# The weights of a two-layer kernel's mixtures: ScalarE issues their loads into six buffers, their splits move among the first scores, and the expert slots are cleared during the first mixtures

## Chip, core and metric

One core of one Trainium2 chip runs the whole program. The metric is the device time of one execution in microseconds. It is given as the median of several executions. Three executions of the kernel before gave 2954.35, 2950.48 and 2947.49 us.

## The reference

The input `x` is (32, 256, 256) float32 with a context of the same shape. There are four sublayers, each a normalisation followed by a block that is added to `x`:

```python
x = x + _L0_xattn_ref(_layernorm(x), ctx, ctx, Wq, bq, Wk, bk, Wv, bv, Wo, bo)   # 16 heads of 16
x = x + _L0_ffn_ref(_layernorm(x), P_w, U1, U2, U3, W1, W2, b2)
x = x + _L1_xattn_ref(_layernorm(x), ctx, ctx)                                   # no projections
x = x + _L1_ffn_ref(_layernorm(x), router_w, w_gate, w_up, w_down, ws_gate_up, ws_down)

def _mixture(inp, C, W):            # called with (x, C1, W1), then (gelu(.), C2, W2)
    for e in range(L):              # L = 12 matrices of 256 x 256
        y = y + C[:, e:e + 1] * (inp @ W[e].T)
```

The last block routes 8192 tokens to 8 of 64 experts. Each expert has 128 slots in a table in DRAM, and a token beyond an expert's capacity is dropped. A slot that nobody fills must read as zeros and must point at a spare output row.

## The kernel before

The 32 batches of 256 rows go through a pipeline that is written out by hand. Every step of a batch has a place on a scale of 40 units per batch (`PLACES`, `MIX`, `HALF_PLACES`). `pieces()` (lines 80 to 112) sorts all steps of all batches by place, and each of the five engines walks that one list and does its share of each step. So the list sets the order of the instructions on each engine, and semaphores keep the engines apart. A place is no time: an engine goes on as soon as what it waits for is there.

Products are done in fp32r with each operand in a high and a low part. For the weights, ScalarE rounds the float32 words to the high part (`split_hi`, line 592), and VectorE subtracts it from the words to get the low part (`split_lo`, line 753). There are 15 chunks of weights: three for the attention (`wo`, `wkv`, `wq`, `FIRST = 3`) and twelve for the mixtures, each two matrices and 128 x 1024 float32 large (512 KB). The raw words of a chunk land in a staging buffer. Two buffers exist: the last two of the five `x_mem` buffers, and `router_mem`. So chunk c is loaded when chunk c-2 has been split (semaphore `v_w`):

```python
def load_chunk(c):                                   # in sync_program, before
    if c >= 2:
        sp.wait_ge(v_w, c - 1)
    sp.e.dma_start(stage[c % 2][:, 0:chunks[c][2]], chunks[c][1]).then_inc(c_stage[c % 2], 16)
```

SyncE issues nearly all transfers of the kernel in the order of the list. Its queue also carries the stores of a batch's keys and queries (`k_parts`, `q_parts`), their rearranged loads (`spread`, from DRAM into `kst` and `qst`), and the four rows of maxima (`qst<-mT`) of each half. The steps `w_mix` (places 1, 3, 5, 11, ... 35) do three things in the kernel before: SyncE loads the next chunk and, for the first eight steps, clears the slots of eight experts by a transfer of 1284 KB (`expert_slots<-row_mem`, line 437), ScalarE splits, VectorE splits.

One half of an attention (8 heads, number `u`) is: `spread`; four `s1` steps (TensorE `first`, VectorE takes their maxima, `nm`, line 846); `max_rows` (VectorE `nmp`, TensorE turns them, ScalarE copies `mT`, SyncE spreads it); four `s2` steps (TensorE `second`, ScalarE `exps`, line 675); two `av` steps; `out_turn` (VectorE writes `ctx_o`). The first half of batch 0 begins at place 2.8 (its `spread`), its `s1` steps at 6.2 to 10.6, and its `s2` steps at 15.4 to 20.5. The mixtures of batch 0 stand at 53 to 88. In batch 1, places are 40 higher.

## Time and profile before

| | |
|---|---|
| median of three executions | 2950.48 us (2947.49 to 2954.35) |
| profiled execution | 2946.47 us, span 2944.7 us |
| TensorE matmuls busy | 2672.1 us, 91% of the span |
| TensorE weight loads | 2250.0 us, 76% |
| VectorE | 2222.4 us, 75% |
| ScalarE | 1060.2 us, 36% |
| GpSimd | 818.0 us, 28% |
| granted TensorE clock, mean over the span | 0.952 |
| moved by DMA | 327.29 MB, 111 GB/s over the span |

The span runs from the first to the last instruction that the profile shows. The time of the execution is 1.8 us longer. The profile's page also cuts the span into 40 slices of 73.6 us: TensorE is busy to 2 and 5 tenths in the first two, and to 9 or more from the third to about the 32nd.

### The profile page before, as it was taken

Reading aid. Unit: us, or ns where it says so; the run is one execution under the profiler, and the core shown is the slowest. Engines: PE = TensorE matmul, PEld = TensorE weight load, DVE = VectorE, ACT = ScalarE, POOL = GpSimd, SP = SyncE. Lnnn points to the kernel's source line nnn. Section 1 sums busy time; section 2 is a strip of 40 time slices with the busy share of each in tenths; the row PEclk is TensorE's granted clock in tenths of the full one; section 3 lists DMA queues with packets and bytes.
Section 4 is the critical chain, followed back from the end, with each engine's and each line's share of the span. In section 5 each row is a group of like instructions: output and inputs, shape, how many; then the busy total and the mean of one; then the engine's idle time right before and its main releaser. Section 6 shows DMA issues by size and latency. Waiting matters only on the chain. (4 is left out here: it accounts for less than half of the span.)

```text
span 2944.7 us, 60947 instructions
## 1 busy us (share of the span) xinstructions
PE 2672.1 (91%) x23496; PEld 2250.0 (76%) x23496; DVE 2222.4 (75%) x6041; ACT 1060.2 (36%) x1557; POOL 818.0 (28%) x862
## 2 busy tenths in 40 slices
PE   2599999999999999999999999999999999756886
PEld 1388888888888888888888888888888887636775
DVE  2478888888888888888888888888888887533332
ACT  1323444444344443444344433344444443211111
POOL 1000122232223322222222222222332222334334
PEclk6599999999999999999999999999999999857998
DMA  7624444444443344334344434333443331227886
GB/s 207 180 73 103 100 127 130 126 122 115 108 106 100 98 103 102 100 94 94 95 102 102 102 102 96 93 96 99 102 98 95 92 84 42 44 37 208 223 218 129
DMA packets 321061, 327.29 MB, mean 111 GB/s; under 512 B 45389, under 2 KB 302111, under 8 KB 320772
## 3 DMA queue, kind: packets, MB, share of 16 engines
q1 hardware_dynamic: 286980, 304.23, 40.3%
q0 software_dynamic: 33792, 19.17, 3.7%
q8 instruction: 186, 3.05, 0.5%
q14 instruction: 103, 0.84, 0.1%
HBM read 182.21 MB, written 212.37 MB: 134 GB/s over the span
## 5 line engine op out<-in xcount | busy, mean ns | idle before, releaser
L675 ACT ACTIVATE exps<-second 128x1024 f32<-128x1024 f32 x512 | 525.6, 1027 | 757.0 <-PE second L1172 732.7
L569 POOL DMA_INDIRECT expert_slots<-row_mem,sidx x512 | 506.9, 990 | 1005.1 <-PE first L1154 670.0
L1252 PE MATMUL mixp<-w_h,r_part_h 128*128 128x256 f32 x3072 | 667.6, 298 | 11.4 <-DVE hid L938 6.5
L846 DVE TENSOR_REDUCE nm<-first 128x4 f32<-128x1024 f32 x508 | 618.6, 1218 | 29.1 <-PE first L1154 25.6
L1252 PE MATMUL mixp<-w_h,r_part_l 128*128 128x256 f32 x3072 | 611.1, 280 | 0.0
L1252 PE MATMUL mixp<-w_l,r_part_h 128*128 128x256 f32 x3072 | 610.7, 280 | 0.0
L1252 PEld LDWEIGHTS mixp<-w_h,r_part_h 128*128 128x128 f32 x3072 | 468.6, 189 | 62.3 <-DVE hid L938 23.5
L1252 PEld LDWEIGHTS mixp<-w_l,r_part_h 128*128 128x128 f32 x3072 | 469.8, 189 | 0.0
L1252 PEld LDWEIGHTS mixp<-w_h,r_part_l 128*128 128x128 f32 x3072 | 469.7, 188 | 0.0
L938 DVE SCALAR_TENSOR_TENSOR x_mem<-mixp,C,x_mem 128x256 f32<-128x256 f32 x768 | 334.4, 477 | 77.6 <-PE mixp L1252 73.2
L938 DVE SCALAR_TENSOR_TENSOR hid<-mixp,C,hid 128x256 f32<-128x256 f32 x704 | 301.4, 476 | 108.4 <-PE mixp L1252 108.1
L1154 PE MATMUL first<-kst,qst 48*128 48x256 f32 x2032 | 238.9, 313 | 58.6 <-DVE nm L846 34.3
L538 POOL TENSOR_TENSOR norm<-norm,minus_half 128x2 f32<-128x2 f32 x128 | 92.0, 719 | 717.9 <-DVE norm L791 717.9
L1188 PE MATMUL attn_out<-exps,vx 128*17 128x256 f32 x4096 | 275.9, 392 | 11.1 <-issue 6.7
L1172 PE MATMUL second<-qst,kst 50*128 50x256 f32 x2048 | 237.4, 310 | 20.1 <-DMA qst<-mT 10.1
L1154 PEld LDWEIGHTS first<-kst,qst 48*128 48x128 f32 x2032 | 157.5, 189 | 111.4 <-DVE nm L846 37.8
L1172 PEld LDWEIGHTS second<-qst,kst 50*128 50x128 f32 x2048 | 159.1, 189 | 77.3 <-issue 30.4
L1188 PEld LDWEIGHTS attn_out<-exps,vx 128*17 128x17 f32 x4096 | 95.5, 98 | 112.1 <-issue 33.9
L582 POOL DMA_INDIRECT out<-x_mem,sidx x64 | 99.2, 1550 | 169.1 <-DVE sidx L1028 117.9
L681 ACT COPY out_sb<-attn_out 128x512 f32<-128x512 f32 x128 | 74.5, 582 | 133.3 <-PE attn_out L1188 117.3
L610 ACT ACTIVATE nat_h<-misc,qk_cols 128x256 fp32r<-128x256 f32 x128 | 53.8, 471 | 157.5 <-PE misc L1125 157.5
L813 DVE TENSOR_SCALAR xhat<-x_mem,norm 128x256 f32<-128x256 f32 x192 | 92.8, 524 | 9.2 <-issue 7.5
(223 smaller groups left out, 3620.0 us busy)
## 6 DMA issues: line engine op xcount, KB each, us to landing
kst<-k_parts SPq DMA_DIRECT2D x256, 192.0 KB
qst<-q_parts SPq DMA_DIRECT2D x256, 192.0 KB
q_parts<-nat_h SPq DMA_DIRECT2D x128, 256.0 KB
k_parts<-ctx_part_h SPq DMA_DIRECT2D x64, 256.0 KB
k_parts<-nat_h SPq DMA_DIRECT2D x64, 256.0 KB
q_parts<-nat_l SPq DMA_DIRECT2D x64, 256.0 KB
exps<-in_wgu SPq DMA_DIRECT2D x39, 384.0 KB
expert_slots<-row_mem SPq DMA_DIRECT2D x8, 1284.0 KB, 10.7
```

The source lines that it names most:

```text
L538: pool.e.tensor_tensor(rstd[kind][:, :], veps[kind][:, :], minus_half[:, :], ALU.pow).then_inc(p_pow[kind], 1)
L569: pool.e.indirect_dma_start(out=slots_dram, out_offset=bass.IndirectOffsetOnAxis(ap=sidx[b % 2][:, t, k:k + 1], axis=0), in_=row[b % 2][:, ...
L582: pool.e.indirect_dma_start(out=out_pad, out_offset=bass.IndirectOffsetOnAxis(ap=eid[e % NID], axis=0), in_=ey[e % NY], in_offset=None, bo ...
L675: act.e.activation(exps[:, j % NU, :, :, :].rearrange("p k t s -> p (k t s)"), second[:, :, :].rearrange("p k s -> p (k s)"), ACT.Exp, sca ...
L681: act.e.copy(out_sb[:, :, :].rearrange("p g s -> p (g s)"), attn_out[:, :]).then_inc(a_out, 1)
L813: dve.e.tensor_scalar(dst[:, t, 0:D], src[:, t, :], mv[kind][:, t, 0:1], rstd[kind][:, t:t + 1], ALU.subtract, ALU.mult).then_inc(v_norm[k ...
L846: dve.e.tensor_reduce(nm[u % 2][:, :, 2 * j:2 * j + 2].rearrange("p t k -> p k t"), (mixp_mem if in_mixp(b, kind, j) else first)[:, :, :]. ...
L938: dve.e.scalar_tensor_tensor(acc, src, c, acc, ALU.mult, ALU.add).then_inc(v_mix, 1)
L1154: m = pe.e.matmul(bank[k][:, t * S:(t + 1) * S], q_st[u % 3][at, j, t * P:(t + 1) * P], k_st[u % 3][at, j, :], start=True, stop=True)
L1172: m = pe.e.matmul(bank2[k][:, s * S:(s + 1) * S], k_st[u % 3][at, j, s * P:(s + 1) * P], q_st[u % 3][at, j, :], start=True, stop=True)
L1188: m = pe.e.matmul(attn_out[r0:r0 + HD + 1, q * S:(q + 1) * S], vx[:, s, h * H // 2 + HQ * q + i, :], exps[:, (2 * q + i // 2) % NU, i % 2, ...
L1252: m = pe.e.matmul(mixp[q % 2][:, t * D:(t + 1) * D], src[i][:, dt, t * P:(t + 1) * P], wmix[n][j][:, l, dt, :], start=(k == 0), stop=(k == ...
```

## The change

ScalarE issues the loads of the twelve chunks of the mixtures. There are six staging buffers: the two old ones and the four buffers of `exps`. The first three loads wait for nothing, the next three for one split each, and the rest are issued ahead of a split, five chunks ahead of it. The `w_mix` steps move to places -15 to 12. The first exponential waits until all 15 chunks are split, since it writes `exps`. The sum of the biases, which had lain in `exps`, lies in `out_sb`. Clearing the slots becomes a step of its own, `empty`: 16 transfers of four experts each, at places 68 to 120.5, still issued by SyncE. The diff, with its smaller places left out:

```diff
-EMPTIED = 8
+EMPTIED = 4
...
-W_MIX = tuple(10 * s + 1 + 2 * k for s in range(4) for k in range(3))
+EMPTY = tuple(68 + 3.5 * i for i in range(16))
+W_MIX = (-15, -13, -11, -9, -6, -3, 2, 4.5, 7, 8.5, 10, 12)
...
-    placed = [(p, ("w_mix", i)) for i, p in enumerate(W_MIX)]
+    placed = [(p, ("w_mix", i)) for i, p in enumerate(W_MIX)] + [(p, ("empty", i)) for i, p in enumerate(EMPTY)]
...
-        b_raw = exps_flat[0:2, 0:D]
         out_sb = sb("out_sb", (P, 2, S))
+        b_raw = out_sb[0:2, 0, :]
...
+        stage += [exps_flat[:, i * 2 * DT * D:(i + 1) * 2 * DT * D] for i in range(4)]
+        NS = len(stage)
...
-            def load_chunk(c):
-                if c >= 2:
-                    sp.wait_ge(v_w, c - 1)
-                sp.e.dma_start(stage[c % 2][:, 0:chunks[c][2]], chunks[c][1]).then_inc(c_stage[c % 2], 16)
-
             for c in range(FIRST):
-                load_chunk(c)
-            emptied = 0
+                sp.e.dma_start(stage[c][:, 0:chunks[c][2]], chunks[c][1]).then_inc(c_stage[c], 16)
...
-                elif what == "w_mix":
-                    load_chunk(FIRST + a[0])
-                    if emptied < NE:
-                        sp.wait_ge(p_const, 1)
-                        sp.e.dma_start(slots[:, emptied:emptied + EMPTIED, :],
-                                       empty_rows.unsqueeze(1).broadcast_to([P, EMPTIED, ROW])).then_inc(c_init, 16)
-                        emptied += EMPTIED
-                        if emptied >= NE:
...
+                elif what == "empty":
+                    n = a[0] * EMPTIED
+                    sp.wait_ge(p_const, 1)
+                    sp.e.dma_start(slots[:, n:n + EMPTIED, :],
+                                   empty_rows.unsqueeze(1).broadcast_to([P, EMPTIED, ROW])).then_inc(c_init, 16)
+                    if n + EMPTIED == NE:
...
             def split_hi(c):
-                act.wait_ge(c_stage[c % 2], 16 * (c // 2 + 1))
-                act.e.copy(chunks[c][0][0], stage[c % 2][:, 0:chunks[c][2]]).then_inc(a_w, 1)
+                act.wait_ge(c_stage[c % NS], 16 * (c // NS + 1))
+                act.e.copy(chunks[c][0][0], stage[c % NS][:, 0:chunks[c][2]]).then_inc(a_w, 1)
+
+            def load_chunk(c):
+                if c >= NS:
+                    act.wait_ge(v_w, c - NS + 1)
+                act.e.dma_start(stage[c % NS][:, 0:chunks[c][2]], chunks[c][1]).then_inc(c_stage[c % NS], 16)
...
             for c in range(FIRST):
                 split_hi(c)
+                load_chunk(FIRST + c)
+            for c in range(FIRST):
+                load_chunk(2 * FIRST + c)
...
                 if what == "w_mix":
-                    split_hi(FIRST + a[0])
+                    c = FIRST + a[0]
+                    if NS + FIRST <= c + NS - 1 < CHUNKS:
+                        load_chunk(c + NS - 1)
+                    split_hi(c)
...
-                    act.wait_ge(v_b, 1)
+                    act.wait_ge(v_w, CHUNKS)
                     act.e.activation(exps[:, j % NU, :, :, :].rearrange("p k t s -> p (k t s)"),
...
+                    act.wait_ge(v_b, 1)
                     act.e.copy(out_sb[:, :, :].rearrange("p g s -> p (g s)"), attn_out[:, :]).then_inc(a_out, 1)
```

How it moves instructions is seen best at three places. The names in brackets are the semaphores that a row waits for. First SyncE's queue, from the reload of `ctxT` to the spreads of the first two halves, before:

```order
L364 DMA router_mem<-in_w1T 128x1024 [waits dve_w]
L437 DMA expert_slots<-row_mem 128x8x321 [waits pool_const]
L368 DMA q_parts<-nat_h 128x2x256 [waits dve_q]
L368 DMA q_parts<-nat_l 128x2x256
L368 DMA q_parts<-nat_h 128x2x256
L416 DMA kst<-k_parts 48x4x256 [waits pool_const,k_parts_out]
L416 DMA kst<-k_parts 48x4x256
L419 DMA qst<-q_parts 48x4x256 [waits q_parts_out]
L419 DMA qst<-q_parts 48x4x256
L416 DMA kst<-k_parts 48x4x256 x2
L419 DMA qst<-q_parts 48x4x256 x2
L364 DMA x_mem<-in_w1T 128x1024 [waits dve_w]
```

and with the change:

```order
L385 DMA ctxT<-in_ctxT 128x2x256
L366 DMA q_parts<-nat_h 128x2x256 [waits dve_q]
L366 DMA q_parts<-nat_l 128x2x256
L366 DMA q_parts<-nat_h 128x2x256
L413 DMA kst<-k_parts 48x4x256 [waits pool_const,k_parts_out]
L413 DMA kst<-k_parts 48x4x256
L416 DMA qst<-q_parts 48x4x256 [waits q_parts_out]
L416 DMA qst<-q_parts 48x4x256
L413 DMA kst<-k_parts 48x4x256 x2
L416 DMA qst<-q_parts 48x4x256 x2
```

The chunks and the clearing of slots are gone from between the stores and the spreads, and no row waits for `dve_w` here.

Second ScalarE, from batch 0's queries to the first exponential, before (`a_part_h` and `nat_h` are batch 0's queries, `mT` the maxima of its first half):

```order
L606 CAST a_part_h<-misc 128x512 [waits pe_qt]
L610 ACTIVATE nat_h<-misc,qk_cols 128x256 [waits k_parts_out,pe_q]
L610 ACTIVATE nat_h<-misc,qk_cols 128x256
L594 CAST w_h<-router_mem 128x1024 [waits stage_in1]
L594 CAST w_h<-x_mem 128x1024 [waits stage_in0]
L594 CAST w_h<-router_mem 128x1024 [waits stage_in1]
L594 CAST w_h<-x_mem 128x1024 [waits stage_in0]
L669 CAST mT<-misc 16x256 [waits pe_mx]
L594 CAST w_h<-router_mem 128x1024 [waits stage_in1]
L638 COPY vx<-misc 128x32x16 [waits dve_zero,pe_v]
L594 CAST w_h<-x_mem 128x1024 [waits stage_in0]
L675 ACTIVATE exps<-second 128x1024 [waits dve_b,pe_s2]
```

and with the change, its piece from batch 0's keys to the queries' `nat_h` and just behind:

```order
L589 CAST w_h<-exps 128x1024 [waits stage_in3]
L594 DMA exps<-in_w2T 128x1024 [waits dve_w]
L589 CAST w_h<-exps 128x1024 [waits stage_in4]
L594 DMA exps<-in_w2T 128x1024 [waits dve_w]
L589 CAST w_h<-exps 128x1024 [waits stage_in5]
L609 CAST a_part_h<-misc 128x512 [waits pe_qt]
L594 DMA exps<-in_w2T 128x1024 [waits dve_w]
L589 CAST w_h<-x_mem 128x1024 [waits stage_in0]
L613 ACTIVATE nat_h<-misc,qk_cols 128x256 [waits k_parts_out,pe_q]
L613 ACTIVATE nat_h<-misc,qk_cols 128x256
L594 DMA x_mem<-in_w2T 128x1024 [waits dve_w]
L589 CAST w_h<-router_mem 128x1024 [waits stage_in1]
```

Splits and loads now stand ahead of and between the steps of the queries, and each load there waits for a VectorE split (`dve_w`). The splits of the last six chunks follow, the last one just behind `mT`.

Third SyncE in the mixtures, from the maxima of half 6 to the spread of half 8, before (batches and halves are counted from 0; halves 8 and 9 are the first attention of batch 3):

```order
L427 DMA qst<-mT 1x4x256 [waits act_mT]
L427 DMA qst<-mT 1x4x256 x3
L388 DMA ctxT<-in_ctxT 128x2x256 [waits pool_v]
L368 DMA q_parts<-nat_h 128x2x256 [waits dve_q]
L368 DMA q_parts<-nat_l 128x2x256
L368 DMA q_parts<-nat_h 128x2x256
L416 DMA kst<-k_parts 48x4x256 [waits pe_s2,k_parts_out]
L416 DMA kst<-k_parts 48x4x256
L419 DMA qst<-q_parts 48x4x256 [waits q_parts_out]
```

and with the change:

```order
L424 DMA qst<-mT 1x4x256 [waits act_mT]
L424 DMA qst<-mT 1x4x256 x3
L433 DMA expert_slots<-row_mem 128x4x321 x2
L385 DMA ctxT<-in_ctxT 128x2x256 [waits pool_v]
L433 DMA expert_slots<-row_mem 128x4x321
L437 DMA out<-row_mem 128x256 x2
L366 DMA q_parts<-nat_h 128x2x256 [waits dve_q]
L366 DMA q_parts<-nat_l 128x2x256
L366 DMA q_parts<-nat_h 128x2x256
L413 DMA kst<-k_parts 48x4x256 [waits pe_s2,k_parts_out]
L413 DMA kst<-k_parts 48x4x256
L416 DMA qst<-q_parts 48x4x256 [waits q_parts_out]
```

Three clearings and the two transfers into the spare output rows (L437) now stand ahead of the stores of batch 3's queries, which the next spread reads.

## Rows read from the trace of the kernel before

**Rows 1.** Stretches: us, busy time of the engines, granted clock (PEclk), DMA share, GB/s.

```profile
20.00:40.00 20.00, 6.19 (x28) 5.39 (x27) 4.31 (x8) 3.31 (x6) 0.61 (x1) 0.66 0.84 245
40.00:60.00 20.00, 2.03 (x12) 1.44 (x12) 4.81 (x4) 2.09 (x2) 0.00 (x0) 0.50 1.07 272
60.00:80.00 20.00, 5.98 (x30) 4.33 (x28) 5.07 (x6) 3.56 (x5) 0.00 (x0) 0.50 0.74 226
...
1000.00:2000.00 1000.00, 979.67 (x8996) 824.49 (x8997) 859.34 (x2324) 409.02 (x579) 291.12 (x315) 1.00 0.40 98
```

**Rows 2.** Waits of TensorE, 20 to 160 us: total us, times, longest.

```profile
PE first L1154 <- DVE nm L846: 32.9, 8, 13.8
PE first L1154 <- DMA qst<-q_parts: 16.8, 2, 12.6
...
PE misc L1083 <- DVE ctx_o L869: 4.8, 2, 4.0
```

**Rows 3.** Timeline of ScalarE: start, us, line, operation, count, idle before and releaser.

```profile
16.77 0.62 ACT L594 CAST wq_h<-x_mem 128x512 fp32r<-128x512 f32 x1 [2.53 <-DMA x_mem<-in_wqT]
...
25.87 0.59 ACT L606 CAST a_part_h<-misc 128x512 fp32r<-128x512 f32 x1 [2.36 <-PE misc L1083]
...
48.17 1.04 ACT L594 CAST w_h<-x_mem 128x1024 fp32r<-128x1024 f32 x1 [15.39 <-DMA x_mem<-in_w1T]
...
79.38 1.04 ACT L594 CAST w_h<-x_mem 128x1024 fp32r<-128x1024 f32 x1 [4.76 <-DMA x_mem<-in_w1T]
80.33 1.02 ACT L675 ACTIVATE exps<-second 128x1024 f32<-128x1024 f32 x1
```

**Rows 4.** Timeline of VectorE, weight splits and what follows them.

```profile
49.25 1.23 DVE L755 TENSOR_TENSOR w_l<-x_mem,w_h 128x1024 fp32r<-128x1024 f32 x1 [15.21 <-ACT w_h L594]
...
64.80 0.17 DVE L856 CAST nmp<-nm 128x16 fp32r<-128x16 f32 x1
...
81.60 1.22 DVE L846 TENSOR_REDUCE nm<-first 128x4 f32<-128x1024 f32 x1
...
91.01 1.22 DVE L755 TENSOR_TENSOR w_l<-router_mem,w_h 128x1024 fp32r<-128x1024 f32 x1 [1.19 <-ACT w_h L594]
...
108.81 1.23 DVE L755 TENSOR_TENSOR w_l<-router_mem,w_h 128x1024 fp32r<-128x1024 f32 x1 [6.01 <-ACT w_h L594]
...
110.23 0.42 DVE L869 TENSOR_TENSOR ctx_o<-misc,rsum 128x256 f32<-128x256 f32 x1
```

**Rows 5.** Timeline of TensorE: first `s1`, first `s2`, first `s1` of batch 1.

```profile
42.81 0.79 PE L1154 MATMUL first<-kst,qst 48*128 48x256 f32 x4 [12.64 <-DMA qst<-q_parts]
...
69.87 0.80 PE L1172 MATMUL second<-qst,kst 50*128 50x256 f32 x4
...
131.56 0.80 PE L1154 MATMUL first<-kst,qst 48*128 48x256 f32 x4 [4.13 <-DMA qst<-q_parts]
```

**Rows 6.** Timeline of SyncE's queue: start of issue and its duration.

```profile
31.98 0.37 SPq L368 DMA_DIRECT2D q_parts<-nat_h  x1
...
41.37 0.44 SPq L364 DMA_DIRECT2D x_mem<-in_w1T  x1
...
43.51 6.62 SPq L382 DMA_DIRECT2D x_mem<-in_x  x1
...
66.12 2.59 SPq L427 DMA_DIRECT2D qst<-mT  x4
...
120.26 0.38 SPq L368 DMA_DIRECT2D q_parts<-nat_h  x1
...
225.26 0.79 SPq L419 DMA_DIRECT2D qst<-q_parts  x2
```

**Rows 7.** DMA issues up to 150 us: count, KB each, median us to landing.

```profile
expert_slots<-row_mem SPq DMA_DIRECT2D x8, 1284.0 KB, 10.7
```

**Rows 8.** Waits of TensorE for DMA, 300 to 2300 us.

```profile
PE second L1172 <- DMA qst<-mT: 1.5, 4, 0.5
```

**Rows 9.** Timeline of TensorE: first `s1` of half 6.

```profile
234.31 0.50 PE L1154 MATMUL first<-kst,qst 48*128 48x256 f32 x4
```

More of the change, by code:

```diff
@@ L278, in build @@
         c_w, c_init, c_add = sem("weights_in"), sem("slots_init"), sem("combine")
-        c_stage = sems("stage_in", 2)
+        c_stage = sems("stage_in", NS)
         c_x = sems("x_in", 2)
@@ L432, in sync_program @@
                     sp.e.dma_start(out_rows(b), X[b % NXB][:, :, :]).then_inc(c_out[b % 2], 16)
-                elif what == "w_mix":
-                    load_chunk(FIRST + a[0])
-                    if emptied < NE:
-                        sp.wait_ge(p_const, 1)
-                        sp.e.dma_start(slots[:, emptied:emptied + EMPTIED, :],
-                                       empty_rows.unsqueeze(1).broadcast_to([P, EMPTIED, ROW])).then_inc(c_init, 16)
-                        emptied += EMPTIED
-                        if emptied >= NE:
-                            for i in range(2):
-                                sp.e.dma_start(out_pad[T + i * P:T + (i + 1) * P, :], empty_rows[:, 0:D]).then_inc(c_init, 16)
+                elif what == "empty":
[4 more added lines that the diff above has]
+                    if n + EMPTIED == NE:
+                        for i in range(2):
+                            sp.e.dma_start(out_pad[T + i * P:T + (i + 1) * P, :], empty_rows[:, 0:D]).then_inc(c_init, 16)
                 elif what == "e_turn":
@@ L754, in split_lo @@
                 dve.wait_ge(a_w, c + 1)
-                dve.e.tensor_tensor(chunks[c][0][1], stage[c % 2][:, 0:chunks[c][2]], chunks[c][0][0].bitcast(F32),
+                dve.e.tensor_tensor(chunks[c][0][1], stage[c % NS][:, 0:chunks[c][2]], chunks[c][0][0].bitcast(F32),
                                     ALU.subtract).then_inc(v_w, 1)
```

## The prediction

> **What bounds the kernel now.** I read the stretches first. From 1000 to 2000 us TensorE's matmuls are busy 979.7 of 1000 us at full granted clock, and the DMA share is 0.40 [rows 1]. In that part nothing but TensorE's own work counts. The first stretches differ: in 40 to 60 us TensorE works 2.0 us and in 60 to 80 us 6.0 us, at a granted clock of 0.50 (the level of 1.2 GHz; it had idled for most of that time), while the DMA share is 1.07 and 0.74 [rows 1]. So the start is held by something else, and time won there moves everything behind it forward.
>
> Next the waits of TensorE from 20 to 160 us: 32.9 us for VectorE's maxima `nm`, in 8 waits with 13.8 us the longest, and 16.8 us for queries from DRAM, 12.6 of it for the first [rows 2]. VectorE's timeline says why the maxima are late. It follows the list, and weight splits stand ahead of them: one waited 15.2 us for ScalarE's half of the split [rows 4]. ScalarE in turn waited 15.39 us for the chunk itself, and the next waits are of the same kind, down to 4.76 us ahead of the split at 79.38, behind which the first exponential stood [rows 3]. The chunk of 48.17 was issued at 41.37, behind stores, spreads and a clearing of 1284 KB, though its buffer had been free from soon after the split of 16.77 [rows 3]; SyncE then stood 6.62 us in one issue, its queue full [rows 6]. The first exponential comes at 80.33, though TensorE's first `s2` was there at 69.87 [rows 3, 5].
>
> **The change, step by step.** The sum goes by the profiled execution (2946.5 us); the median is 4.0 us above it.
>
> *Up to batch 0's keys: 0.* The third attention chunk has its own buffer, so ScalarE's wait of 2.53 us for it goes [rows 3]. In its place ScalarE issues six loads. The nearest row is SyncE's issue of such a chunk, 0.44 us [rows 6], so 2.6 us in all. Bounds: -2.5 us if an issue lies beside the copy running on the engine, +3 us if an issue with a full queue costs as much as 43.51 shows in part. I take 0.
>
> *Queries of batch 0: +4.7 us.* Three mixture splits now stand on ScalarE ahead of `a_part_h`, and the loads between them wait for VectorE's split. That is 2 x (1.04 + 1.23 + 0.44) + 1.04 = 6.5 us [rows 3, 4, 6], of which 2.36 us lie in the idle time that ScalarE had there before `a_part_h` [rows 3]. VectorE then finishes its third split about 0.6 us after the copy and does the queries' low part only then. So 6.5 - 2.4 + 0.6 = 4.7. Bounds 0 (issues and splits overlap wholly) and +7. Who waits: TensorE's projection, SyncE's stores, and the first spread. From the first store to the first `s1` it took 10.8 us (31.98 to 42.81), and in batch 1, where no clearing was in the queue, 11.3 us (120.26 to 131.56) [rows 5, 6]; I keep 10.8. First `s1` at 47.5 instead of 42.8.
>
> *First scores: -12.1 us.* From the first `s1` to the maxima's `nmp` it took 22.0 us (42.81 to 64.80) [rows 4, 5]. Now VectorE has four reductions of 1.22 and three splits of 1.23 between them [rows 4], 8.6 us, with 0.8 us of TensorE ahead and some 0.5 us of handing over: 9.9 us. This needs the chunks there on time; ScalarE needs at most 2.7 us for each of the four that stand between the queries and the first `s1`, 10.8 us, which is what the stores and the spread take. First `nmp` at 57.4.
>
> *To the first exponential: -9.6 us.* Before, 15.5 us (64.80 to 80.33). Now 1.3 us to SyncE's issue, 3.75 us from there to the first `s2` (66.12 to 69.87) and 0.9 us of TensorE: 5.9 us [rows 3 to 6]. The new wait for all 15 splits lies beside it: the last split stands behind `nmp` and ends at about 58.9. The first exponential comes at 63.3, 17.0 us earlier. If the last chunk lands after 60, this wait is what is late next.
>
> *The rest of the first attention: -7 us.* The reduction at 81.60 started after the exponential and can now start before it, and the split at 91.01 no longer delays `nmp` (behind a reduction that had ended 1.2 us earlier): 3.0 us together. The split at 108.81, whose chunk VectorE had awaited for 6.01 us, stood ahead of `ctx_o` at 110.23, for which TensorE waited up to 4.0 us [rows 2]; I take 3.2 us of it. One exponential stood behind a split for 0.8 us. Bounds 0 and -10 (3 us more, for the other two splits that follow in this part) [rows 4].
>
> *Clearing the slots: +1.5 us.* In the first 100 us its eight transfers are gone: 8 x 1284 KB; that gain is in the terms above. They return as 16 of 642 KB between half 4 and half 8, with the DMA share at 0.40 before. By 10.7 us to landing for 1284 KB [rows 7] one is 5.35 us, a bound from above, since that row holds time in the queue. The rate of 272 GB/s [rows 1] gives 2.4 us. Most are issued while SyncE waits for the next maxima, and drain before those. At three places one could show. One clearing stands ahead of the spread of half 6, issued at 225.26 and needed at 234.31 [rows 6, 9]: 2.4 us fit into it. Two, with a load and a store of keys, stand behind the maxima of half 5 and may reach the next ones. Three and the two spare blocks stand ahead of batch 3's stores, some 9 us of transfers in front of a spread with about 8 us of slack. TensorE's waits for the maxima are 1.5 us in 2000 us, in 4 waits of 0.5 us or less [rows 8], so these rows sit with little slack. Bounds 0 and 16 x 5.35 = 86; I take 1.5, near the lower end, by the slack of the second row.
>
> *Moved at no cost:* the biases' sum in `out_sb` and the waits for it lie ahead of ScalarE's `wq_h` at 16.77 [rows 3], where its wait for the chunk covers them; without that cover they cost what they cost before.
>
> The sum: 0 + 4.7 - 12.1 - 9.6 - 7.0 + 1.5 = -22.5 us. The profiled execution would take 2924.0 us, the median 2928.0 us.
>
> **Rivals.** *(a) The start becomes bound by DMA traffic.* From 20 to 80 us 14.9 MB moved [rows 1]; without six clearings (7.9 MB) and with six more chunks (3.1 MB) 10.1 MB must move before the first exponential. At 245 to 272 GB/s that is 37 to 41 us, up to 61 us at the latest, just inside the forecast. But the chunks now run beside the stores and spreads, not behind them. If the first spread takes twice the 4.2 us that it takes now and the last chunks 3 us longer, 7 us of the gain go: 2935 us. For it: the share was already 1.07. Against: the clearings are gone from just there. Rows of one queue can't show that.
>
> *(b) Slower: clearings exposed in the TensorE-bound part.* There 1 us of a late spread is 1 us of the end. If half of the 5.35 us of each of the 16 showed, 43 us would be lost: 2950.5 - 24.0 + 43 = 2969 us. The point from which it decides is 24 / 16 = 1.5 us per clearing. For it: little slack at the maxima [rows 8]. Against: half of the traffic's room is free [rows 1].
>
> *(c) The gain isn't passed on.* ScalarE's issues prove long, as at 43.51, and take back what the order gives: twelve issues with 2 us more each make 24 us, so 2950 us. The same skill page says (section on issuing engines) that starting DMAs from several engines saves only the time that it takes to start them. By it alone the change would be worth the twelve issues of SyncE, 12 x 0.44 = 5.3 us, so 2945 us. The waits of 15.39 us for a chunk that stood behind spreads in the order speak against it.
>
> **How the numbers follow.** Forecast 0.72, (a) 0.18, (b) 0.04, (c) 0.06. The predicted time is the forecast's, 2928 us. The bounds of the terms add up to some 14 us on the fast side (keys -2.5, queries -4.7, rest -3.4, clearing -1.5, and 2 for the measurement): 2914. On the slow side (a) with the clearing at 6 us and 2 for the measurement gives 2942. Together 8 in 10. A measurement of this kernel can tell about 0.2%, 5.9 us, from no change. Faster by more than that: forecast, (a) and a part of (c), 0.92. Within it: 0.04. Slower: (b), 0.04.
>
> **What would show it.** In the new profile the first `s1` should stand at 46 to 49 us, the first `nmp` at 56 to 59, the first exponential at 62 to 65, and the first `s1` of batch 1 at 105 to 109 instead of 131.56. ScalarE's waits for chunks should be near zero, and TensorE's waits for `nm` up to 160 us under 15 instead of 32.9. From 200 us on each step should be 22 to 24 us earlier. If first `s1` comes after 52, (a) holds; if the lead shrinks between 150 and 260 us by more than 3 us, the clearings are exposed; if single ScalarE issues last over 1 us, (c). A first exponential after 68 or a last one no earlier than before would make the prediction wrong.

## The result, and the profile after

| | before | after |
|---|---|---|
| median | 2950.99 us (2947.49 to 2954.35, 6 executions) | 2927.89 us (2924.97 to 2931.61, 6 executions) |
| ratio after / before | | 0.9922, 95% interval 0.9911 to 0.9932 |
| profiled execution | 2946.47 us | 2931.61 us |
| span, mean granted clock | 2944.7 us, 0.952 | 2929.8 us, 0.957 |
| TensorE matmuls busy | 2672.1 us | 2673.7 us |

The changed kernel is 23.1 us faster; 22.5 us and 2928.0 us were forecast. The profiled execution of the changed kernel is the slowest of its six. At 2460 us its lead was 22.2 us and at the experts' first load 26.3 us (2658.50 to 2632.20). From that load to the end it took 297.6 us, against 286.2 us in the profiled execution before, and 293.6 us in a second profile of the changed kernel (2636.92 to 2930.5). The change touches nothing there. The traces of the other experiments show how far this last part scatters: in all fourteen profiles it takes 286.2 to 298.0 us, and the kernel before has the shortest. In the three kernels that are the one before with only places or clearings moved it took 292.8, 294.0 and 294.5 us. So I take these 7 to 11 us for the scatter of single executions, with 286.2 us its fast end. I compare the start by landmarks, and the end by medians.

The stretches, of the kernel after; columns as in [rows 1]:

```profile
20.00:40.00 20.00, 6.25 (x27) 5.28 (x26) 9.68 (x13) 8.21 (x11) 0.00 (x0) 0.95 0.82 267
40.00:60.00 20.00, 3.18 (x16) 2.01 (x16) 10.47 (x10) 4.93 (x5) 0.00 (x0) 0.50 0.74 153
60.00:80.00 20.00, 13.71 (x80) 9.75 (x80) 9.33 (x18) 8.09 (x12) 1.97 (x2) 0.59 0.13 42
...
200.00:220.00 20.00, 17.90 (x180) 14.33 (x178) 13.90 (x32) 9.53 (x13) 0.74 (x2) 1.00 0.90 205
220.00:240.00 20.00, 19.55 (x180) 17.45 (x176) 15.23 (x29) 8.50 (x12) 0.56 (x1) 1.00 0.80 252
1000.00:2000.00 1000.00, 980.23 (x9012) 824.77 (x9011) 860.26 (x2329) 405.46 (x575) 291.27 (x315) 1.00 0.40 98
```

From 60 to 80 us TensorE works 13.7 us instead of 6.0, and the DMA share there has fallen from 0.74 to 0.13. The clearings are now issued between 144 and 233 us, and from 200 to 240 us the DMA share is 0.90 and 0.80. The middle of the kernel is as it was.

TensorE's waits from 20 to 160 us, of the kernel after:

```profile
PE first L1161 <- DMA qst<-q_parts: 20.4, 2, 16.8
PE first L1161 <- DVE nm L853: 9.2, 8, 1.5
PE misc L1132 <- DVE a_part_l L769: 6.0, 1, 6.0
```

Against [rows 2] the eight waits for the maxima fell from 32.9 to 9.2 us (under 15 was forecast). The waits for queries grew by 3.6 us, and a new one appeared, for the low part of the queries' operand (`a_part_l`), which VectorE writes only behind the three splits that now stand ahead of it.

ScalarE's timeline, of the kernel after (start, duration, line, operation, count, idle before and its releaser):

```profile
13.35 0.42 ACTq L594 DMA_DIRECT2D exps<-in_w1T  x1
13.80 1.04 ACT L589 CAST wkv_h<-router_mem 128x1024 fp32r<-128x1024 f32 x1
14.65 0.34 ACTq L594 DMA_DIRECT2D x_mem<-in_w1T  x1
...
28.90 1.04 ACT L589 CAST w_h<-exps 128x1024 fp32r<-128x1024 f32 x1 [1.66 <-DVE w_l L762]
29.85 0.58 ACT L609 CAST a_part_h<-misc 128x512 fp32r<-128x512 f32 x1
...
61.73 1.04 ACT L589 CAST w_h<-exps 128x1024 fp32r<-128x1024 f32 x1
64.84 0.59 ACT L644 COPY vx<-misc 128x512 f32<-128x512 f32 x1 [2.07 <-PE misc L1144]
66.15 1.02 ACT L681 ACTIVATE exps<-second 128x1024 f32<-128x1024 f32 x1 [0.72 <-PE second L1179]
```

Its own issues (ACTq) last 0.33 to 0.42 us, and the one of 14.65 is issued before the copy of 13.80 to 14.84 has ended. It hardly waits for chunks: the waits of 15.39 and 4.76 us of [rows 3] are gone. The first exponential stands at 66.15 instead of 80.33.

VectorE between the first scores, of the kernel after:

```profile
52.47 1.23 DVE L853 TENSOR_REDUCE nm<-first 128x4 f32<-128x1024 f32 x1 [8.05 <-PE first L1161]
53.61 1.22 DVE L762 TENSOR_TENSOR w_l<-exps,w_h 128x1024 fp32r<-128x1024 f32 x1
54.74 1.22 DVE L853 TENSOR_REDUCE nm<-first 128x4 f32<-128x1024 f32 x1
55.88 1.22 DVE L762 TENSOR_TENSOR w_l<-x_mem,w_h 128x1024 fp32r<-128x1024 f32 x1
57.01 1.22 DVE L853 TENSOR_REDUCE nm<-first 128x4 f32<-128x1024 f32 x1
58.14 1.22 DVE L762 TENSOR_TENSOR w_l<-router_mem,w_h 128x1024 fp32r<-128x1024 f32 x1
59.27 1.22 DVE L853 TENSOR_REDUCE nm<-first 128x4 f32<-128x1024 f32 x1
60.53 0.17 DVE L863 CAST nmp<-nm 128x16 fp32r<-128x16 f32 x1
```

Reductions and splits now alternate without a gap: 8.06 us from the first to `nmp`, where a single wait was 15.21 us in [rows 4]. But the row of 52.47 had an idle time of 8.05 us in front of it. TensorE and SyncE say why, of the kernel after (two views, the landmarks that answer to [rows 5] and [rows 6]):

```profile
51.63 0.80 PE L1161 MATMUL first<-kst,qst 48*128 48x256 f32 x4 [16.84 <-DMA qst<-q_parts]
...
109.06 0.79 PE L1161 MATMUL first<-kst,qst 48*128 48x256 f32 x4 [3.54 <-DMA qst<-q_parts]
```

```profile
36.60 0.36 SPq L366 DMA_DIRECT2D q_parts<-nat_h  x1
...
44.72 1.08 SPq L416 DMA_DIRECT2D qst<-q_parts  x2
...
226.97 2.44 SPq L424 DMA_DIRECT2D qst<-mT  x4
229.45 0.99 SPq L433 DMA_DIRECT2D expert_slots<-row_mem  x2
```

From the first query store to the first `s1` it took 15.0 us (36.60 to 51.63), against 10.8 before. The first `s1` of batch 1 is 22.5 us earlier (109.06 against 131.56), and half 6's row of maxima, which SyncE issued at 249.35 in the kernel before, is 22.4 us earlier. That is the lead that stays: the clearings on either side of it have cost nothing so far. TensorE has no wait for a DMA between 120 and 300 us, and from 300 to 2300 us those for `qst<-mT` are 1.2 us in 3 waits (in [rows 8] 1.5 in 4).

Each step as forecast and as measured:

| step | forecast | measured |
|---|---|---|
| first query store (31.98 to 36.60) | +4.7 | +4.6 |
| from it to the first `s1` (10.8 to 15.0) | 0 | +4.2 |
| to the first `nmp` (22.0 to 8.9) | -12.1 | -13.1 |
| to the first exponential (15.5 to 5.6) | -9.6 | -9.9 |
| to the first `s1` of batch 1 (51.2 to 42.9) | -7.0 | -8.3 |
| from there to half 6's maxima, clearings between (117.8 to 117.9) | +1.5 (for all 16) | +0.1 |
| sum | -22.5 | -22.4 |

### The profile page after: what moved, and what is told of

Read it like the earlier page. It is cut to its first block and busy times, and to the rows that moved or that the text cites. A ratio compares the mean times of both kernels' runs of the same rounds, so it can differ in the third digit from the quotient of the medians.

```text
span 2929.8 us, 60955 instructions
## 1 busy us (share of the span) xinstructions
PE 2673.7 (91%) x23496; PEld 2250.8 (77%) x23496; DVE 2222.5 (76%) x6041; ACT 1060.3 (36%) x1557; POOL 818.0 (28%) x862
## 5 line engine op out<-in xcount | busy, mean ns | idle before, releaser
L1259 PE MATMUL mixp<-w_h,r_part_h 128*128 128x256 f32 x3072 | 667.1, 298 | 11.4 <-DVE hid L945 6.5
L1195 PE MATMUL attn_out<-exps,vx 128*17 128x256 f32 x4096 | 275.9, 391 | 10.4 <-issue 6.8
```

What stands on the lines that cost most here:

```text
L1195: m = pe.e.matmul(attn_out[r0:r0 + HD + 1, q * S:(q + 1) * S], vx[:, s, h * H // 2 + HQ * q + i, :], exps[:, (2 * q + i // 2) % NU, i % 2, ...
L1259: m = pe.e.matmul(mixp[q % 2][:, t * D:(t + 1) * D], src[i][:, dt, t * P:(t + 1) * P], wmix[n][j][:, l, dt, :], start=(k == 0), stop=(k == ...
```

## The experiments

Twelve runs were made, in four sessions of which each has its own executions of the kernel before. One session ran on a chip where the kernel before took 2927.87 us, so kernels of different sessions are compared by their ratios. (The lead at half 6 is against the one trace of the kernel before also for these, since no other was taken.) Two numbers describe each: the lead of half 6's maxima over 249.35 us, from its trace, and the gain in medians. "Store" is the first query store, "exp" the first exponential.

| kernel | store | first `s1` | `nmp` | exp | lead at half 6 | median gain | ratio (95%) |
|---|---|---|---|---|---|---|---|
| after | 36.60 | 51.63 | 60.53 | 66.15 | 22.4 | 23.1 | 0.9922 (0.9911 to 0.9932) |
| after, again | 36.13 | 50.71 | 59.61 | 65.25 | 23.2 | 21.4 | 0.9920 (0.9903 to 0.9936) |
| before + clearing late | 32.87 | 42.11 | 60.16 | 70.27 | 13.7 | 14.4 | 0.9949 (0.9932 to 0.9966) |
| before + new places | 55.40 | 75.80 | 99.87 | 109.17 | -22.7 | -21.8 | 1.0063 (1.0047 to 1.0080) |
| before + both | 41.74 | 52.50 | 70.48 | 79.78 | 8.3 | 5.7 | 0.9974 (0.9961 to 0.9987) |
| after, clearing early | 50.85 | 73.59 | 82.49 | 88.13 | 1.5 | 3.3 | 0.9991 (0.9982 to 1.0001) |
| after, SyncE issues | 40.22 | 52.71 | 61.61 | 67.53 | 20.7 | 21.7 | 0.9923 (0.9907 to 0.9940) |
| after, two buffers | 40.00 | 55.33 | 69.77 | 75.39 | 13.4 | 19.0 | 0.9925 (0.9909 to 0.9942) |
| the same, again | 39.56 | 52.53 | 66.14 | 72.06 | 16.1 | 17.5 | 0.9940 (0.9927 to 0.9952) |
| after, clearing twice | 35.88 | 49.91 | 58.81 | 64.73 | 16.7 | 11.1 | 0.9957 (0.9941 to 0.9974) |
| after, late loads small | 35.92 | 45.30 | 54.19 | 60.10 | 27.7 | 28.7 | 0.9899 (0.9886 to 0.9913) |
| after, splits behind the queries | 31.44 | 49.11 | 58.00 | 63.92 | 26.2 | 26.1 | 0.9914 (0.9901 to 0.9926) |
| after, last loads held | 31.94 | 45.90 | 57.28 | 62.90 | 26.6 | 25.4 | 0.9909 (0.9892 to 0.9925) |

With one exception, the lead at half 6 is the gain at the end to within 3 us for each kernel whose clearings are no more than the change's; the exception is the first run with two buffers (13.4 and 19.0, its executions 2927.76 to 2939.61). So what is won in the first 230 us is what is won.

**The change once more.** No edit.

> The changed kernel once more, as the measure for the others of this chip. Both theories: 22 to 24 us under the kernel before, first exponential at 66 us, first scores of batch 1 at 109 us, no step of 140 to 260 us later than its lead of 22.4 us allows.

The medians are 2932.61 us and 2953.98 us for the kernel before: 21.4 us, just under the 22 expected, and the ratio repeats. The landmarks repeat within 1 us, and the stretch from store to `s1` within 0.5 us (14.6).

**The clearing alone moved.**

```diff
-EMPTIED = 8
+EMPTIED = 4
+EMPTY = tuple(68 + 3.5 * i for i in range(16))
...
-                    if emptied < NE:
...
+                elif what == "empty":
```

> The kernel before with the clearing of the slots alone moved (16 transfers of four experts at places 68 to 120.5); loads still by SyncE into two buffers at the old places. Theory (the order of splits and loads is what costs at the start, the clearings only stretch single waits for a chunk): 6 to 10 us under the kernel before, first exponential at 70 to 75 us. Rival (the clearings' traffic is what held the start, so that moving them is most of the change): 18 us or more under it, first exponential at 62 to 66 us.

14.4 us: between the two, a little nearer to the rival. The first exponential at 70.27 is where the theory had it. The wait for the chunk behind the spreads stayed, as its row shows; ScalarE's timeline of this kernel:

```profile
48.01 1.04 ACT L594 CAST w_h<-x_mem 128x1024 fp32r<-128x1024 f32 x1 [15.15 <-DMA x_mem<-in_w1T]
...
67.90 1.04 ACT L594 CAST w_h<-router_mem 128x1024 fp32r<-128x1024 f32 x1 [6.45 <-DMA router_mem<-in_w1T]
```

So of the 15.39 us of [rows 3] the list's order made nearly all. The clearing's share lies before (`s1` 0.7 us earlier) and above all behind it: the first exponential comes 10.1 us earlier.

**The new places alone**, two buffers, SyncE's loads and clearings as before.

```diff
-W_MIX = tuple(10 * s + 1 + 2 * k for s in range(4) for k in range(3))
+W_MIX = (-15, -13, -11, -9, -6, -3, 2, 4.5, 7, 8.5, 10, 12)
```

> The kernel before with the new places of the splits alone; loads by SyncE into two buffers at those steps, eight of them with a clearing of 1284 KB behind them. Theory (order and number of buffers belong together): all twelve chunks must now go through two buffers ahead of the first exponential, at about 6 us for each with a clearing in the same queue, so the first exponential comes at 85 to 105 us and the time is 0 to 15 us over the kernel before. Rival (the places alone bring the gain): 10 us or more under it.

21.8 us slower, more than the theory's upper end of 15 (the first exponential, at 109.17, is past its 105 too), and the rival fell. The clearings move with the splits, ahead of the first queries; SyncE's queue of this kernel:

```profile
34.72 0.46 SPq L437 DMA_DIRECT2D expert_slots<-row_mem  x1
35.22 5.84 SPq L368 DMA_DIRECT2D k_parts<-nat_h  x2
...
55.40 5.17 SPq L368 DMA_DIRECT2D q_parts<-nat_h  x1
```

**Both in the kernel before** (the two edits above together).

> The kernel before with the new places and the late clearing; loads still by SyncE into two buffers. Theory: about 4 us for each of twelve chunks (5 us to land, splits of 2.3 us, two buffers in turn), first exponential at 68 to 75 us, time 12 to 18 us under the kernel before, so that six buffers and ScalarE's issues are worth 5 to 10 us of the 23. Rival (six buffers and ScalarE's queue carry the change): less than 8 us under the kernel before.

5.7 us: the rival's, and the first exponential at 79.78 is later than the theory's 75. The new places cost 8.7 us against the clearing alone (14.4), as long as there are two buffers and every load waits for a split. The first store comes at 41.74 instead of 32.87.

**Clearing put back to the start of the changed kernel**, eight transfers of 1284 KB at the first eight split steps.

```diff
-EMPTIED = 4
+EMPTIED = 8
...
-                elif what == "empty":
+                elif what == "w_mix" and a[0] < NE // EMPTIED:
```

> The changed kernel with the clearing put back: eight transfers of 1284 KB by SyncE at the first eight split steps (new places -15 to 4.5). Theory (moving the clearing alone gave 14 us, because 10.5 MB leave the start): the 10.5 MB return, now all ahead of the first scores; at 270 GB/s they take 39 us, part of it in idle queue time: first scores after 65 us instead of 51, time 15 to 35 us over the changed kernel. Rival (with six buffers and a queue of ScalarE's own for the chunks, clearings on SyncE's queue disturb the chunks no more): less than 8 us over it.

Only 3.3 us are left of 23.1, as the theory had it. SyncE's queue of this kernel shows it standing in its issues:

```profile
20.98 13.86 SPq L432 DMA_DIRECT2D expert_slots<-row_mem  x4
34.88 4.42 SPq L365 DMA_DIRECT2D k_parts<-nat_h  x2
...
40.29 5.45 SPq L432 DMA_DIRECT2D expert_slots<-row_mem  x2
...
50.85 8.79 SPq L365 DMA_DIRECT2D q_parts<-nat_h  x1
```

**SyncE issues the chunks**, into the same six buffers: the last six at the same steps, the first three right behind the attention's chunks, the next three behind the stores of the context's keys.

```diff
-                act.e.dma_start(stage[c % NS][:, 0:chunks[c][2]], chunks[c][1]).then_inc(c_stage[c % NS], 16)
+                sp.e.dma_start(stage[c % NS][:, 0:chunks[c][2]], chunks[c][1]).then_inc(c_stage[c % NS], 16)
...
+            for c in range(FIRST, 2 * FIRST):
+                load_chunk(c)
...
+                    for c in range(2 * FIRST, 3 * FIRST):
+                        load_chunk(c)
```

> The changed kernel with all loads of chunks issued by SyncE: three behind the attention's chunks, three behind the stores of the context's keys, the rest at the split steps; six buffers, same places. Theory (buffers matter, not who issues): the three loads of w_mix steps ahead of the stores of the queries' parts make SyncE wait for VectorE's splits, so the stores of keys and queries come up to 2 us later, but chunks no longer run beside the first spread: within 3 us of the changed kernel. Rival (ScalarE's own queue is what matters, since SyncE's is in order): 6 us or more over it.

0.9923, the changed kernel's own ratio; the lead at half 6 is 1.7 us less, which the medians can't tell. With six buffers and late clearings, which queue the loads are on is not what the change wins by. That is what the Trainium skill says on "DMA: Bandwidth & Descriptors", section "Issuing engines are not separate DMA queues": a second issuing engine saves only the time of issuing. This pair of runs agrees, as far as its interval (0.9907 to 0.9940, some 5 us either way) can tell.

Inside the start the issuer does move time. The first store comes 3.6 us later (2 were expected), and the stretch from it to `s1` is 12.5 us instead of 15.0. SyncE's queue, now the only one with work, was busy for 86.5% of it, 10.8 us for 3.13 MB, where the two queues of the changed kernel had 15.2 us of packet time for 3.59 MB. So packet time depends on what runs side by side; why, was not tried.

**Two buffers in the changed kernel**, run in two sessions.

```diff
-        stage += [exps_flat[:, i * 2 * DT * D:(i + 1) * 2 * DT * D] for i in range(4)]
...
-                    if NS + FIRST <= c + NS - 1 < CHUNKS:
+                    if FIRST + NS <= c + NS - 1 < CHUNKS:
```

> The changed kernel with two staging buffers only, loads still issued by ScalarE, each waiting for the split two chunks back. Theory (the number of buffers carries the second half of the gain): a chunk takes (0.4 + 5 + 1.0 + 1.2) / 2 = 3.8 us, so twelve take 46 us, last split at 62 to 68 us, queries 3 to 5 us later, first exponential at 69 to 75 us: 4 to 9 us over the changed kernel. Rival (ScalarE's queue alone does it, buffers don't count): within 2 us of it.

By time this fell to the rival (0.9925), but its executions were 12 us apart and its landmarks 9 us behind, so it decides nothing. It ran again:

> Two staging buffers with ScalarE's issues once more, since four times between 2927.8 and 2939.6 us left it open whether six buffers count. Theory (they do: its profile had the first exponential at 75.4 us and half 6's maxima 9.8 us later than the changed kernel): ratio to the kernel before 0.9935 to 0.9955, 5 to 9 us over the changed kernel. Rival (the delay is absorbed further down): ratio 0.992 to 0.993, as the changed kernel.

0.9940 against 0.992: 5 to 6 us of a kernel of 2928 us, as the theory had it. The intervals of the two ratios still overlap; the landmarks are clearer, with 6.3 us less lead at half 6 than the changed kernel in this run and 9.0 in the first. VectorE's timeline of this second run shows where:

```profile
53.37 1.23 DVE L853 TENSOR_REDUCE nm<-first 128x4 f32<-128x1024 f32 x1 [0.19 <-PE first L1161]
57.51 1.22 DVE L762 TENSOR_TENSOR w_l<-router_mem,w_h 128x1024 fp32r<-128x1024 f32 x1 [2.92 <-ACT w_h L590]
58.65 1.22 DVE L853 TENSOR_REDUCE nm<-first 128x4 f32<-128x1024 f32 x1
60.94 1.23 DVE L762 TENSOR_TENSOR w_l<-x_mem,w_h 128x1024 fp32r<-128x1024 f32 x1 [1.07 <-ACT w_h L590]
```

The splits between the reductions are late again, behind ScalarE's halves (13.6 us from `s1` to `nmp`, not 8.9).

**Clearing twice.** Each of the 16 late transfers is followed by one of the same size into a second table that nobody reads.

```diff
+                    for rows in (slots, twin):
-                    sp.e.dma_start(slots[:, n:n + EMPTIED, :],
+                        sp.e.dma_start(rows[:, n:n + EMPTIED, :],
```

> The changed kernel with each of the 16 late clearings issued a second time, into another table that nobody reads: 21 MB instead of 10.5 between 140 and 240 us. Theory (the late clearings fit into slack): the slack is small, DMA share was 0.7 to 0.9 in four of the six stretches of 20 us there; 3 to 12 us over the changed kernel, seen as waits of TensorE for qst<-q_parts and qst<-mT between 140 and 260 us. Rival (ample room): within 1.5 us of it.

0.9957: some 11 us lost against the changed kernel, inside the theory's range. The stretches of this kernel show the DMA engines full or nearly so:

```profile
200.00:220.00 20.00, 18.95 (x169) 16.59 (x170) 16.32 (x38) 6.17 (x9) 1.17 (x2) 1.00 0.97 274
220.00:240.00 20.00, 14.82 (x150) 11.46 (x150) 9.61 (x18) 8.87 (x11) 0.61 (x1) 1.00 1.09 264
240.00:260.00 20.00, 18.19 (x160) 15.53 (x160) 15.84 (x35) 6.37 (x9) 0.69 (x1) 0.91 1.00 279
```

At half 6 the lead is 16.7 us, and the next half's maxima are 14.5 us behind those of the changed kernel (258.30 to 243.81): the second 10.5 MB no longer fit beside TensorE's work. The first do, by the +0.1 us above. From 140 to 300 us TensorE waits 10.1 us for DMAs here (6.4 for queries, 3.7 for a row of maxima), and not at all in the changed kernel.

**Late loads small.** Of the last three chunks only 64 of 1024 columns are loaded, so these weights are left out and old words are split in their place.

```diff
+                n = chunks[c][2] if c < 12 else 64
-                act.e.dma_start(stage[c % NS][:, 0:chunks[c][2]], chunks[c][1]).then_inc(c_stage[c % NS], 16)
+                act.e.dma_start(stage[c % NS][:, 0:n], chunks[c][1][:, 0:n]).then_inc(c_stage[c % NS], 16)
```

> The changed kernel whose last three chunk loads bring 64 of 1024 columns (the rest of those chunks' weights is left over from earlier chunks). Theory (the first spread is late because it shares the DMA engines with ScalarE's last loads): stores of the queries at 36 us as before, first scores at 47 to 49 us instead of 50.7 to 51.6, time 2 to 4 us under the changed kernel. Rival (the spread is late because of the spread of the next half and of its own small rows, not the chunks): first scores after 50 us, within 1 us of the changed kernel.

The first `s1` came at 45.30, earlier than forecast, 9.4 us behind the store; the ratio is 0.9899, which is 6 to 7 us better than the changed kernel's, where 2 to 4 were expected. What the DMA queues carried between store and first `s1` explains the size. First the changed kernel from 36.60 to 51.63 us, then this one from 35.92 to 45.30 (queue: packets, MB, share of 16 engines in that time; q1 is SyncE's, q10 ScalarE's):

```profile
q1 hardware_dynamic: 2215, 2.12, 67.1%
q10 hardware_dynamic: 407, 1.47, 33.8%
```

```profile
q1 hardware_dynamic: 1923, 1.84, 94.7%
q10 hardware_dynamic: 288, 0.07, 5.1%
```

Together the shares are 101% and 100%: the 16 engines were busy nearly throughout in both. (A share can pass 100%; in the kernel before it reads 109.1% from 40.5 to 42.8 us. So it doesn't prove that nothing more would fit.) ScalarE's part is 33.8% of 15.0 us, 5.1 us, and 5.1% of 9.4 us, 0.5 us. The difference, 4.6 us, is most of the 5.6 us by which the stretch is shorter, and a little more than the 4.2 us by which the forecast missed. The rest of it is SyncE's own (10.1 us against 8.9). The three stores and the four transfers of the first spread are 1.57 MB; what lies above that in SyncE's 2.12 and 1.84 MB is not needed by the first `s1`, being part of the next half's spread and of a load of `x`, so a longer stretch also takes in more of it.

**Splits behind the queries.** Chunks 3 to 7 are split after the queries' part, and each load is issued one split later.

```diff
-W_MIX = (-15, -13, -11, -9, -6, -3, 2, 4.5, 7, 8.5, 10, 12)
+W_MIX = (-6.2, -6.1, -6, -5.8, -5.6, -3, 2, 4.5, 7, 8.5, 10, 12)
...
-                    if NS + FIRST <= c + NS - 1 < CHUNKS:
+                    if NS + FIRST <= c + NS - 2 < CHUNKS:
```

> The changed kernel with the first five split steps moved behind the queries (places -6.2 to -5.6) and each later load issued one split later, so that ScalarE doesn't wait for VectorE's split at hand. Theory (the queries' path to DRAM sets the first scores, splits have room while the spread is under way): stores of the queries at 31 to 33 us instead of 36.4, first scores at 43 to 48 us, all eight splits ahead of them done by 46 to 50 us, first exponential at 60 to 63 us, time 3 to 6 us under the changed kernel. Rival (the traffic of stores, spreads and chunks sets the first scores, whatever the order): first scores at 50 to 52 us again, within 1.5 us of the changed kernel.

The store came 5.2 us earlier, at 31.44, but the first `s1` only 2.5 us: all six loads now fell into the stretch, and it took 17.7 us. In it ScalarE's queue held the larger share of the engines:

```profile
q10 hardware_dynamic: 854, 3.12, 59.0%
q1 hardware_dynamic: 1829, 1.75, 39.5%
```

59.0% of 17.7 us are 10.4 us. SyncE's 1.75 MB took 7.0 us here, while its 1.84 MB took 8.9 us with the late loads small: the packet time of the same kind of transfer is no fixed price. Of the theory only the store came true; the first `s1` (49.11, expected 43 to 48), the first exponential (63.92, expected 60 to 63) and the time missed its ranges, and `s1` came before the rival's 50. The ratio of 0.9914 is not told from the changed kernel's; the lead at half 6 is 3.8 us more.

**Last loads held**, the attempt at a better version: the edit above, and the last three loads wait for TensorE's first `s1`.

```diff
-                    if NS + FIRST <= c + NS - 2 < CHUNKS:
+                    if NS + FIRST <= c + NS - 2 < CHUNKS - FIRST:
...
+                    if c == CHUNKS - FIRST - 1:
+                        act.wait_ge(t_s1, 1)
+                        for k in range(CHUNKS - FIRST, CHUNKS):
+                            load_chunk(k)
```

> The changed kernel with three edits: the splits of chunks 3 to 7 stand behind the queries, as in the run before; of the six later loads only three (chunks 9 to 11) are issued beside the stores and the spread; the last three wait on ScalarE for TensorE's first `s1`, so that the first spread has the DMA engines nearly to itself. Theory (the later chunks' loads are what made the stretch from the first query store to the first `s1` long: 15.0 us in the changed kernel, 17.7 with all six loads behind the queries, 9.4 without most of the last three): store at about 31.5, first `s1` at 42 to 44 (store to `s1` 10.5 to 12.5), the first exponential 15 to 17 us behind it (57 to 60; the last chunk has some 10 us from its load to its split), half 6's maxima 6 to 9 us earlier than in the changed kernel, ratio to the kernel before 0.989 to 0.990, 2 to 3 us per thousand better than the changed kernel's 0.992. Rival (the stretch is long for SyncE's own transfers, the stores, keys, queries and inputs that follow each other on one queue, and the loads matter little): store to `s1` stays above 15 us, first `s1` after 46.5. A second rival: the last three loads come too late for their splits, then the first exponential follows `s1` by over 19 us and the ratio is 0.991 or more.

14.0 us from store to `s1`, between theory (10.5 to 12.5) and rival (over 15). The lead at half 6 grew by 4.3 us where 6 to 9 were expected, and the ratio missed its range of 0.989 to 0.990. The three loads that stayed still lay in the stretch with 34.8% of the engines (4.9 us). And the held chunks came late; ScalarE's timeline of this kernel:

```profile
47.60 0.44 ACTq L594 DMA_DIRECT2D exps<-in_w2T  x1
51.54 1.04 ACT L589 CAST w_h<-x_mem 128x1024 fp32r<-128x1024 f32 x1 [6.27 <-DMA x_mem<-in_w2T]
```

That put 2.5 us between `s1` and `nmp` (11.4 instead of 8.9). What holding won on one side it lost on the other: the lead at half 6 is 26.6 us against 26.2 without it. The ratio, 0.9909, is the best of a kernel that computes everything, but its interval holds the changed kernel's. No version is shown to beat it.

## Why the prediction was right

The total came out, and with it the gain from the new order of the splits, the shorter waits for `nm`, and the room for the clearings in the middle. The first landmarks did not: `s1` at 51.63 (46 to 49 was forecast), `nmp` at 60.53 (56 to 59), the first exponential at 66.15 (62 to 65), and `s1` of batch 1 at 109.06 (105 to 109). One term is to blame for the first three, the stretch from the first store to the first `s1`. Term by term:

*Up to the keys, 0:* right. The first part of the context starts at 17.11 us instead of 17.51, and ScalarE's six issues lie partly beside its copies.

*Queries of batch 0, +4.7:* measured +4.6, and by the splits as counted: with them behind the queries the store came at 31.44 us instead of 36.60. But the term kept the 10.8 us from store to `s1` unchanged, and this was mis-sized: it measured 15.0 us. The DMA engines are busy nearly throughout this stretch, and the packet time that the loads put into it goes most of the way to explain its length. In the kernel before, SyncE's queue alone filled it (100.9% of 10.8 us), with some of the clearing; without clearing and nearly without loads it is 9.2 us (the clearing alone moved: 97.4%, one queue). The change takes the clearing out and puts 5.1 us of loads in. The term went by the row of batch 1 (11.3 us, no clearing) and put nothing down for the loads, though the text on rival (a) knew that they would run beside the stores and spreads. That row was itself no measure of an empty stretch: in the changed kernel batch 1 has neither a clearing nor a chunk load in it and still takes 10.9 us (98.15 to 109.06). This is rival (a)'s mechanism at some 60% of its size: (a) put 4.2 us on the spread and 3 us on the last chunks. The first came, the second didn't; VectorE's split of the last chunk, at 62.80 us, lay past the 60 that the prediction feared and delayed nothing. The first `s1` came at 51.63, just short of the 52 from which (a) was to hold. Half of each engine, which (a) gave to SyncE while ScalarE's loads last, is not what the traces show where both have work: from 43.0 to 49.1 us of "splits behind the queries", SyncE's queue had 29.4% and ScalarE's 75.2%, with 513 packets (0.48 MB) against 369 (1.32 MB). The packets were of like number; ScalarE's were larger.

*First scores, -12.1:* -13.1. Four reductions and three splits in a row, as counted, with 0.84 us for TensorE ahead instead of 0.8, and less for handing over.

*To the first exponential, -9.6:* -9.9. The wait for all 15 splits lay beside other work, as said.

*The rest of the first attention, -7.0:* -8.3, within its bounds.

*Clearing, +1.5:* +0.1 at half 6, and the medians leave no room for more at the end. Its lower bound was the truth, but doubling the transfers costs 11 us, so it isn't free by a wide margin. Rival (b) fell.

*The sum* is right because one term that was 4.2 us too good stood against three that were 1.0, 0.3 and 1.3 us and one that was 1.4 us too bad: +4.2 - 4.0. That is partly luck, and the landmarks tell it, the total doesn't. The range was not the sum of the terms' bounds either: the fast side has 3.4 us for the rest of the first attention where its bound gives 3.0, and the slow side leaves out the terms' own upper bounds (3 us for the keys, 2.3 for the queries, 7 for the rest of the first attention).

*Rival (c):* ScalarE's issues last 0.33 to 0.42 us. It fell, and so did the estimate of 2945 us by the Trainium skill's rule alone. (The prediction calls SyncE's queue full at 43.51. The profile shows only how long an issue lasts, 6.62 us there, and not how full a queue is.) The rule itself is not hurt by that, since the gain comes from the order, the six buffers and the clearing, and who issues the loads changes nothing that the medians show.

What each part is worth, by the runs: moving the clearing 14.4 us by itself and 19.8 us in the changed kernel (23.1 - 3.3). The new places cost 8.7 us with two buffers on SyncE. Four more buffers, at ScalarE's steps, give 1 to 6 us by the ratios of the two sessions and 6 to 9 us in lead at half 6. What lies between "both in the kernel before" (5.7 us) and "two buffers" of the changed kernel (17.5 to 19.0 us) is 12 to 13 us, the largest part beside the clearing, and it was not taken apart: there the loads leave SyncE's list, the first ones start earlier, and the biases' sum moves. So which of these brings it stays open. Nor was it tried whether ScalarE's queue counts when the clearings are early.

## What to carry to other kernels

Where a stretch has the DMA engines full, add up the packet time of everything that lies in it: in these runs a load that only a later step needs cost the earlier one most or all of its own time (with 4.4, 4.6 and 9.9 us more of loads than with the late loads small, the stretch was 4.6, 5.6 and 8.3 us longer). Such a sum is good to 1 or 2 us with the same two queues, and it doesn't carry over to another order: with SyncE issuing, nearly the same bytes took 2.5 us less. Take out first what nobody needs soon (here 10.5 MB of clearing, worth 14.4 us by itself and 19.8 in the changed kernel), and put it where TensorE is the bound, after counting what fits. More buffers pay where splits stand between steps that others wait for, and a check of single landmarks finds errors that cancel in the total.

## What was not expected of the hardware

- An issue can stand for many times its usual length. With the clearing put back to the start, SyncE was in four clearings of 1284 KB for 13.86 us, in the two stores behind them for 4.42, in two more clearings for 5.45 and in one store of queries for 8.79 us, where the same store is issued in 0.36 us in the changed kernel; with the late loads small, such stores had landed 2.7 us (median) after their issue. In the kernel before the longest near there was 6.62 us [rows 6]. On one queue all that is behind such an issue waits, needed or not.
- Bytes alone are the wrong measure of a transfer here. With the late loads small, SyncE's stores (36.6 to 39.2 us) moved 0.31 MB per us of packet time and the spreads (40.5 to 45.3 us) 0.15, both in packets of about 1 KB; ScalarE's chunk loads moved 0.29 (1.47 MB in 5.1 us), in packets of about 3.6 KB. So a spread is about twice as dear as a store or a chunk load of its size. What makes it so (its 48 partitions, reading from DRAM in small packets) was not tried.
